# Weighted sums of two tiles in every odd step, none in even ones: a token tower's attention loop

## What is computed

```python
def reference(x, ...):
    h = tok(x, ...)                       # embedding, 6 x (conv, gate), projection
    h = h + attn(layernorm(h), ...)
    h = h + ffn(layernorm(h), ...)
    return h

# attn, 8 heads of 16 columns, L = 1024
attn1 = softmax(q1 @ k1.T * scale); attn2 = softmax(q2 @ k2.T * scale)
gate_in = concat(window_stats(attn1, ws), window_stats(attn2, ws))   # mean, std, max, min
alpha = sigmoid(mlp(gate_in))
fused = alpha_full * attn1 + (1 - alpha_full) * attn2
out = (fused @ v) @ Wo
```

## Time and profile before

| what | value |
|---|---|
| median of 3 runs | 6056.63 us (6050.68 to 6056.67) |
| profiled execution, span from first to last instruction | 6159.6 us |
| the span less the runs' median | 103 us |
| mean granted TensorE clock | 0.942 |

### The profile page before, as it was taken

The page is one execution under the profiler, slowest core; times in us unless marked ns, Lnnn a source line. Parts: engine busy times, 40 slices in busy tenths (PEclk is TensorE's granted clock), DMA queues, the critical chain, the costliest instruction groups (busy, mean ns, idle before and its releaser), DMA issues.

```text
span 6159.6 us, 116651 instructions
## 1 busy us (share of the span) xinstructions
PE 5323.7 (86%) x34070; PEld 2463.4 (40%) x34070; DVE 5116.9 (83%) x5665; ACT 5198.9 (84%) x7937; POOL 2450.5 (40%) x4439
## 2 busy tenths in 40 slices
PE   6988989889898988889889898988889889898985
PEld 4443424334343443434334343443434334343442
DVE  1988889888888988889888888988888888888982
ACT  2988889889898988889889897888888889898884
POOL 6525344352433425344252433425344252433422
PEclk8999999999999999999999999999999999999997
DMA  1001010010101001010010101001010010101000
GB/s 38 19 21 26 18 28 20 21 26 22 26 19 27 20 20 26 19 28 19 21 26 22 26 19 27 20 21 26 22 26 18 22 25 22 26 19 27 20 21 12
DMA packets 164901, 140.60 MB, mean 23 GB/s; under 512 B 89197, under 2 KB 108269, under 8 KB 164141
## 3 DMA queue, kind: packets, MB, share of 16 engines
q1 hardware_dynamic: 159100, 124.09, 8.8%
q0 software_dynamic: 4352, 8.92, 0.7%
q10 hardware_dynamic: 816, 0.02, 0.0%
HBM read 21.26 MB, written 8.91 MB: 5 GB/s over the span
## 4 chain that ended last, share of the span: by engine, by line
PE 54%; issue 14%; DVE 13%; ACT 10%; POOL 5%; SPq 1%; another core or an unknown queue 1%; ACTq 0%; DMA 0%; DVEq 0%; POOLq 0%
PE ps_w L387 21%; PE ps_t L387 11%; PE ps_o L387 11%; PE ps_s L387 10%; DVE rowmin L715 7%; ACT junk L577 4%; DVE negmax L710 4%; ACT exps L583 2%; SPq L328 1%; DVE bn L727 1%; ACT hpre L632 1%; DVE o_raw L723 1%; ACT stage L587 1%; POOL part L855 1%
## 5 line engine op out<-in xcount | busy, mean ns | idle before, releaser
L710 DVE TENSOR_REDUCE negmax<-ps_s 128x1 f32<-128x1024 f32 x2048 | 2491.5, 1217 | 805.8 <-PE ps_s L387 695.9
L577 ACT ACTIVATE junk<-ps_s,negmax 128x1024 bf16<-128x1024 f32 x2048 | 2295.5, 1121 | 288.8 <-DVE rowmin L715 278.3
L715 DVE TENSOR_REDUCE rowmin<-ps_s 128x1 f32<-128x1024 f32 x2048 | 2486.7, 1214 | 0.0
L583 ACT ACTIVATE exps<-ps_t 128x1024 f32<-128x1024 f32 x2060 | 2122.3, 1030 | 314.3 <-PE ps_t L387 173.6
L387 PE MATMUL ps_s<-kst,qst 96*128 96x512 bf16 x4096 | 1293.8, 398 | 520.7 <-ACT junk L577 461.4
L387 PE MATMUL ps_o<-exps,v_cur 128*32 128x256 f32 x16512 | 1381.8, 408 | 159.5 <-DVE o_raw L723 130.0
L387 PE MATMUL ps_t<-qst,kst 99*128 99x512 bf16 x4120 | 1305.8, 400 | 85.8 <-ACT exps L583 70.4
L387 PE MATMUL ps_w<-xc,cw 128*128 128x256 f32 x4704 | 1178.6, 387 | 0.0
L387 PEld LDWEIGHTS ps_w<-xc,cw 128*128 128x128 f32 x4704 | 914.3, 195 | 215.4 <-issue 9.5
L855 POOL TENSOR_SCALAR ctmp<-ug 128x256 f32<-128x256 f32 x408 | 165.8, 406 | 1602.8 <-ACT ug L652 1587.4
L387 PEld LDWEIGHTS ps_s<-kst,qst 96*128 96x128 bf16 x4096 | 343.8, 100 | 1106.8 <-ACT junk L577 828.0
(11 more groups left out here) (179 smaller groups left out, 3902.4 us busy)
## 6 DMA issues: line engine op xcount, KB each, us to landing
qst<-part SPq DMA_DIRECT2D x1542, 32.0 KB, 2.0
kst<-part SPq DMA_DIRECT2D x1542, 32.0 KB, 2.0
qst<-mrow SPq DMA_DIRECT2D x1028, 1.5 KB
out_dram<-z SPq DMA_DIRECT2D x17, 512.0 KB, 3.2
fc1s<-in_fc_w SPq DMA_DIRECT2D x17, 256.0 KB
fc2s<-in_fc_w SPq DMA_DIRECT2D x17, 256.0 KB
cw<-in_conv_w SPq DMA_DIRECT2D x1, 2304.0 KB
odif<-in_table,idx POOLq DMA_INDIRECT x136
```

What stands on the lines that cost most here:

```text
L577: nc.scalar.activation(junk[:, n % 2, :], ps_s[:, n % 2, :], ACT.Exp, bias=negmax[:, r, t:t + 1], accum_out=sumsq[:, r, t:t + 1]).then_inc ...
L583: nc.scalar.activation(exps[:, n % RING, :], ps_t[:, :, :].rearrange("p c q -> p (c q)"), ACT.Exp, scale=0.5).then_inc(s_exp, 1)
L710: nc.vector.tensor_reduce(negmax[:, r, t:t + 1], ps_s[:, n % 2, :], axis=AX, op=ALU.max, negate=True)\
L715: nc.vector.tensor_reduce(rowmin[:, r, t:t + 1], ps_s[:, n % 2, :], axis=AX, op=ALU.min)\
```

## The change

In the loop over steps of TensorE's program, the weighted sum of an even step n-1 moves into the following odd step n, directly ahead of that step's own sum. Even steps then issue `scores`, `scores_t` and the side task; odd steps `scores`, two sums, `scores_t` and the side task. What each sum reads, waits for and counts is as before, as are the programs of all other engines and the part behind the loop.

```diff
                     for n in range(STEPS):
                         scores(i, n)
-                        weighted(i, n)
+                        if n % 2:
+                            weighted(i, n - 1)
+                            weighted(i, n)
                         scores_t(i, n)
                         for tk in STEP[n]:
                             task("body", i, tk)
```

## The result

| kernel | median, us | range | runs | ratio (95% interval) |
|---|---|---|---|---|
| before | 6055.9 | 6050.68 to 6061.64 | 10 | |
| after | 6072.07 | 6058.75 to 6081.21 | 10 | 1.0026 [1.0017, 1.0035] |

The change costs 16 us, 0.26%. The forecast was 5957 us. The execution behind the earlier trace rows held some 100 us of idle time that other executions of the same kernel don't have, 64.8 of it the "remote" in the earlier trace rows; what caused it stays open. So the rows of after are set beside those of a second execution of the kernel before (the control, span 6054.9), not beside the earlier trace rows.

The account below looks back on a forecast made before the run. No engine was taken as the bound throughout; what counted was when TensorE gets to the scores. Savings of 70 and 56 us less 24 made 102, scaled by 0.983 to 100: 5957 us, range 5870 to 6065.

Parts of the forecast that it names:

- Fewer changeovers: TensorE switches less between scores and sums: 0.20 us saved per pair, 22 pairs a sequence, 70 us in all.
- The wait for the collection goes: Each unit's first sum no longer waits for VectorE to empty `ps_o`: 3.5 us a sequence, 56 us in all.
- All that gains together: The two forecast savings, from changeovers and from waits for the collection: 70 and 56 us, 126 in all.
- What the odd step pays: Transposed scores start 0.46 later in odd steps, mostly covered by ScalarE slack of some 0.9: 24 us lost.
- Rival 4: Late transposed scores in odd steps cost 33 light pairs 0.37 each, 195 us against 126 gained: 6125 us; chance 0.15.
- Its sign: ScalarE's wait for `ps_t` in odd steps grows well above 12.5 us a sequence while `negmax` idles as before.
- Rival 5: Gaps in lighter even steps drop TensorE to half clock, two more such steps a sequence: 41 us, 5998 us; chance 0.04.
- The ScalarE-filled stretch: 45 us of a sequence where TensorE and ScalarE are both full, 8.5 pairs: no saving from changeovers counted.

Follow-up runs that it names:

- e5: Kernel before, with sums paired only in steps 8j+6 and 8j+7, 16 pairs a sequence, so no sum waits for a collection: 6004.96 us, ratio 0.992.
- e7: Changed kernel, with 14 pairs back in the old order, those whose even step waits and whose odd step holds TensorE work: 6007.84 us, ratio 0.9919.
- e4: Changed kernel, with the two sums moved behind the odd step's transposed scores and side task, except in steps 8j+5: 6075.16 us, ratio 1.0035.
- e6: Changed kernel, with five dense-layer pairs (66/67, 68/69, 72/73, 74/75, 76/77) back in the old order: 6057.12 us, ratio 1.0002.
- e11: Changed kernel plus unread matmuls in TensorE's gaps, 5 in step 22 and 6 in step 110: 6026.93 us, ratio 0.9947.
- e1: Kernel before, with sums paired in only the 24 of 64 odd steps whose pairs had got shorter in the profiles: 5967.38 us, ratio 0.9857.
- e2: Kernel before, with sums paired in only the other 40 odd steps, the complement of e1: 6137.73 us, ratio 1.0139.
- e8: Changed kernel plus unread matmuls in TensorE's gaps, in steps 22 (5), 81 (10), 92 (6) and 110 (6): 5965.46 us, ratio 0.9846.
- e9: Kernel before plus unread matmuls in TensorE's gaps, in steps 22 (5), 81 (10) and 92 (6): 6001.73 us, ratio 0.9911.

## Why the prediction was wrong

**Fewer changeovers: right.** The second sum costs 0.44 (forecast 0.46), the way from scores to transposed scores 0.43 (0.44), a pair gains 0.24 (0.20) where TensorE sets the pace in both steps. The drain that the Trainium skill describes, "TensorEngine Tiling (Array Packing)", Tiling Modes, Key Properties, agrees: the order with half the changeovers kept TensorE busy 65 us less, although some of its sums ran at half clock.

**The wait for the collection goes: right.** It went entirely; pairs of e5 away from half clock gain 0.1 to 0.64, and the kernel gained 52 us in spite of step 23. What part of that is the wait and what part the changeovers in the same pairs, no run tells.

**All that gains together** is 9.7 us a sequence (155 in 16) where 7.9 (126) was forecast, a part of it half clock that moved, as at 94/95.

**What the odd step pays: the step that failed.** Forecast 24 us: five places at 0.3, the rest covered by 0.9 of slack in ScalarE. Measured, the pairs that got longer lose 10.6 a sequence, 170 us. Three things were missed in it.

First, the 0.9 was read in step 107, which has no side task on TensorE. There a delay reaches the others only through `exp_t`, and ScalarE has slack; pair 106/107 is indeed as long as before. Where the odd step has a task, the delay goes through TensorE itself to the next scores, and there is no slack at all. The prediction's own hinted at it: that step, 45, lies in the 35-us stretch that the earlier trace rows gives to VectorE or ScalarE, and yet TensorE has no gap in it. Ten pairs lose 0.22 to 0.51, e7 gives back 64 us with them (48 by their own steps). Rival 4 gave each light pair 0.37, the right size, and took all 33 for such pairs; it put the cause at the late transposed scores. Its sign, a longer wait of ScalarE for them, did come (209.7, now 293.0), but by steps it grew where pairs gained (0.2 to 0.3 in steps 45, 47, 59 and 63) and at half clock (0.9 in step 23, 1.4 in 113), not in eight of the ten light odd steps; and e4, in which they are early, is no faster. In those eight the next scores are late by TensorE's own work; in 57 and 99, where ScalarE waits 0.2 and 0.4 longer, both may have a part.

Second, the dense-layer tasks: even steps there were covered by the sum while ScalarE emptied `ps_w`. The prediction didn't name that wait. 1.0 a sequence, 15 us by e6.

Third, half clock. Rival 5 named the mechanism and its price, 41 us; e11 shows 45, a part of which the kernel before paid too. What was wrong is its chance of 0.04. It rested on no row that shows such a gap, when the even steps that wait longest for ScalarE or VectorE could have been looked up, and the sum in each of them is what the change takes out. Whether the change would be faster without this price is open: e11 is 29 us faster than before, but before had no fill at step 110, where it ran at half clock too.

Measured by themselves the three are 64, 15 and 45 us, at most 124 of the 170; the remainder is half clock that moved between pairs (92/93 +0.74 and 94/95 −1.34, 2/3 +0.78) and so stands on both sides of the account. As the halves e1 and e2 miss the whole by 22 us, none of these shares is good to better than that. Why the clock falls in one gap and not in another, and why step 51 or 94 runs cold when another pair is spared, stays open.

**The ScalarE-filled stretch**, for which nothing was counted, gives next to nothing (steps 66 to 79: +0.6 after, −0.4 where its five dense-layer pairs keep the old order).

## What to carry to other kernels

When work moves between two neighbouring steps, read the pace of each of the two, not that of the stretch: here fewer changeovers paid where TensorE set both, and where another engine set the step that got lighter, the step that got heavier paid in full. Before work is taken out of a gap in TensorE's program, look for what runs behind the gap and at which clock; a gap filled with matmuls that nobody reads can be faster than an empty one. And try a uniform rule by parts: this one was worth −88 us in 24 pairs and +82 in the other 40.

## What the runs showed of the hardware

- Weighted sums of four 32-column blocks: the first behind scores costs 0.57 to the next transposed scores, a second in a row 0.44; two in a row at half clock took 1.94 in place of 1.07.
- Added work that shortens the time: 27 unread matmuls a sequence made after 107 us faster (e8), 21 made before 57 us faster (e9).
- Mean clock says little of what half clock costs. The mean granted clock of after is 0.942, of e11 0.960; as the clock has two levels, that is some 704 us (0.058 / 0.5 of 6066.7) and some 482 us (0.040 / 0.5 of 6028.1) at half clock. Of some 220 us less, 45 reached the end.
